# A CIN recommendation tower on one core: pair products on GpSimd, an accumulating DMA that folds eight fields, and the remainder of c out of PSUM

## The reference

```
e = jnp.stack([tbl_0[ids[:, 0]], ..., tbl_31[ids[:, 31]]], axis=1)   # 512 x 32 x 32
x0 = prev = e
for W in (filter_0, filter_1):
    z = jnp.einsum('bhd,bmd->bhmd', x0, prev).reshape(b, h * m, d)
    prev = relu(jnp.einsum('bpd,pn->bnd', z, W[0]))                  # 128 maps
    outs.append(prev)
z = jnp.sum(jnp.concatenate(outs, axis=1), axis=-1)                  # 512 x 256
h = jnp.concatenate([z, dense_ctx], axis=1)
h = jnp.maximum(h @ W_top1 + b_top1, 0.0)
h = jnp.maximum(h @ W_top2 + b_top2, 0.0)
y = h @ W_top3
```

## Time and profile before

| | |
|---|---|
| median of 3 runs | 1014.85 us (1011.53 to 1015.65) |
| the profiled execution, its own time | 1015.16 us |
| its span in the profile | 1013.4 us |
| mean granted clock of TensorE | 0.965 |
| busy: VectorE, TensorE, ScalarE, GpSimd | 962.2, 914.2, 818.3, 810.8 us |

### The profile page before, as it was taken

How to read it: one execution, slowest core, us unless ns; L and a number is a source line. 1 busy time by engine, 2 the same in 40 slices (tenths; PEclk the granted TensorE clock), 3 DMA queues, 4 the chain that set the end, 5 groups by cost and what they waited for, 6 DMA issues and landing times.

```text
span 1013.4 us, 17901 instructions
## 1 busy us (share of the span) xinstructions
PE 914.2 (90%) x3822; PEld 713.5 (70%) x3822; DVE 962.2 (95%) x1057; ACT 818.3 (81%) x2808; POOL 810.8 (80%) x452
## 2 busy tenths in 40 slices
PE   3989899898999989899999899989899988898998
PEld 2767777777778677677776777767776766677784
DVE  4899999999999999999999999999999999999993
ACT  3878888788888878788888788878888878888892
POOL 5678889788889888889888888888888788896871
PEclk9999999899999989999999899999999999999998
DMA  5412222202222202222211222211222211222000
GB/s 190 133 51 71 71 66 70 59 23 66 71 65 69 69 18 60 70 66 68 69 39 39 70 69 65 70 42 35 71 70 64 69 37 41 70 70 64 1 1 0
DMA packets 42849, 61.18 MB, mean 60 GB/s; under 512 B 6273, under 2 KB 17153, under 8 KB 42786
## 3 DMA queue, kind: packets, MB, share of 16 engines
q1 hardware_dynamic: 38690, 58.48, 18.8%
q0 software_dynamic: 4096, 2.11, 1.4%
HBM read 56.37 MB, written 4.20 MB: 60 GB/s over the span
## 4 chain that ended last, share of the span: by engine, by line
PE 61%; DVE 20%; issue 12%; ACT 3%; POOL 2%; DMA 1%; DVEq 1%; SPq 0%; ACTq 0%; POOLq 0%
PE ps_y L621 17%; PE ps_y L627 17%; PE ps_y L622 16%; DVE csum L514 6%; DVE prod L500 6%; DVE z L474 5%; PE ps_c L608 3%; PE ps_c L609 2%; PE ps_c L610 2%; ACT prod L384 2%; DVE c_lo L479 2%; PE ps_h L632 1%; POOL prod L321 1%; PE ps_c L606 1%; POOL z_lo L310 1%
## 5 line engine op out<-in xcount | busy, mean ns | idle before, releaser
L384 ACT ACTIVATE prod<-ps_y,es 128x128 f32<-128x128 f32 x2560 | 698.8, 416 | 76.2 <-PE ps_y L627 72.6
L321 POOL TENSOR_TENSOR prod<-prod 128x1536 f32<-128x1536 f32 x129 | 450.4, 3491 | 113.6 <-DVE prod L500 96.6
L627 PE MATMUL ps_y<-w_hi,c_lo 128*128 128x512 f32 x1024 | 413.4, 404 | 49.1 <-DVE c_lo L479 49.1
L621 PE MATMUL ps_y<-w_hi,c_hi 128*128 128x512 f32 x1024 | 429.2, 419 | 28.1 <-DVE prod L500 25.0
L622 PE MATMUL ps_y<-w_lo,c_hi 128*128 128x512 f32 x1024 | 411.0, 401 | 0.0
L514 DVE TENSOR_REDUCE csum<-prod 128x64 f32<-128x1280 f32 x256 | 378.2, 1478 | 10.2 <-ACT prod L384 0.6
L474 DVE TENSOR_TENSOR z<-first,second 128x512 f32<-128x512 f32 x160 | 282.1, 1764 | 7.1 <-DMA second<-et_scratch 7.1
L627 PEld LDWEIGHTS ps_y<-w_hi,c_lo 128*128 128x128 f32 x1024 | 198.7, 194 | 105.5 <-DVE c_lo L479 62.0
L500 DVE TENSOR_TENSOR prod<-ps_y,es 128x512 f32<-128x512 f32 x384 | 256.2, 677 | 10.2 <-PE ps_y L627 10.1
L621 PEld LDWEIGHTS ps_y<-w_hi,c_hi 128*128 128x128 f32 x1024 | 198.6, 194 | 94.9 <-DVE prod L500 39.1
L310 POOL TENSOR_TENSOR z_lo<-z,z_hi 128x512 fp32r<-128x512 f32 x155 | 222.3, 1452 | 6.8 <-ACT z_hi L362 6.8
(11 more groups left out here) (59 smaller groups left out, 259.0 us busy)
## 6 DMA issues: line engine op xcount, KB each, us to landing
second<-et_scratch SPq DMA_DIRECT2D x160, 256.0 KB, 4.3
first<-et_scratch SPq DMA_DIRECT2D x32, 256.0 KB, 3.3
et_scratch<-gat SPq DMA_DIRECT2D x64, 64.0 KB
prod<-w SPq DMA_DIRECT2D x4, 512.0 KB, 7.1
gat<-table,rows_now POOLq DMA_INDIRECT x128, 2.4
wt_sb<-wt SPq DMA_DIRECT2D x2, 512.0 KB, 5.5
prod<-w0a SPq DMA_DIRECT2D x1, 320.0 KB, 3.1
prod<-w0b SPq DMA_DIRECT2D x1, 320.0 KB, 3.2
```

Source lines behind the costliest of these rows:

```text
L321: nc.gpsimd.tensor_tensor(high, high, low, ALU.add).then_inc(added, 1)
L384: last = nc.scalar.activation(prod[:, buffer_of(g, u), h // 2, :, h % 2], ps_y[:, bank_of(g, u, k), j * N:(j + 1) * N], ACT.Copy, scale=es ...
L621: nc.tensor.matmul(out, hi, w_hi, start=True, stop=False)
L627: nc.tensor.matmul(out, lo, w_hi, start=False, stop=True).then_inc(y_ready, 1)
```

## The change

Four things are changed.

1. The pair products move from VectorE to GpSimd, placed by a table by tile: chunks 2 and 3 of the next group in tile 0, chunk 4 in tile 1, chunks 0 and 1 of the group after that in tile 3.
2. GpSimd's add is gone. Instead it issues one accumulating DMA a tile, `fold`, which adds fields 0 to 7 onto fields 8 to 15 within `prod`: per partition 4 KB are read and added onto 4 KB, 512 KB in all. It waits for banks 0 to 3 of the tile whose number it stands in, and signals a semaphore of its buffer.
3. The closing sum starts at field 8 and so covers 24 fields.
4. The remainder of c is computed from PSUM as max(ps_c, 0) - c_hi (`rest_c`), before `c` is written. ScalarE writes the whole `c` behind bank 6 of tile 3 (`rectify_whole`), VectorE sums it behind bank 4 of tile 0 of the next group. All of c is now in the order (u, b, d), because the matmuls of layer 1 read z's columns in that order.

```
-ADD = 12
-ADDS_LAST = ((0, 8), (8, 12))
+FOLD = F // 4
...
+        def uses_of_buffer(g, u):
+
+            return g.i * (TG * SLOTS // BUFS) + ((TG * g.r + u) // BUFS + 1)
...
-            def add(g, u, start=0, end=ADD):
...
+            def multiply(g, k):
+
+                pool.wait_ge(pairs_in[k], g.times(32, 32) if k == 0 else g.times(16, 16))
+                wait(pool, z_lo_ready, g.times(KP, k + 1 - KP))
+                nc.gpsimd.tensor_tensor(z[:, k, :], first[:, :], second[:, k, :], ALU.mult).then_inc(z_ready, 1)
+
+            def fold(g, u):
+
+                last_bank = 2 * FOLD // HB - 1
                 pool.wait_ge(act_scaled, signals(ACT_BANKS, g, u, last_bank))
                 pool.wait_ge(dve_scaled, signals(DVE_BANKS, g, u, last_bank))
+                pool.sem_inc(pool_passed, 1)
                 buf = buffer_of(g, u)
-                low, high = prod[:, buf, lows, :, :], prod[:, buf, highs, :, :]
-                nc.gpsimd.tensor_tensor(high, high, low, ALU.add).then_inc(added, 1)
+                pool.dma_start(prod[:, buf, FOLD // 2:FOLD, :, :], prod[:, buf, 0:FOLD // 2, :, :],
+                               accum_op=ALU.add).then_inc(folded[buf], 16)
...
+            Z_AT = {0: ((1, 2), (1, 3)), 1: ((1, 4),), 3: ((2, 0), (2, 1))}
+            Z_LO_AT = {0: (0, 1), 1: (2, 3), 2: (4,)}
...
                 for u in range(TG):
-                    if not (number == 0 and u == 0):
-                        add(*before(g, u))
-                    if u < 2 and (number is None or number + 1 < GROUPS):
-                        split_z(g.plus(1), 2 * u)
-                        split_z(g.plus(1), 2 * u + 1)
-                    if u == 2 and (number is None or number + 1 < GROUPS):
-                        split_z(g.plus(1), LASTK)
+                    products = (Z_AT_FIRST if number == 0 else Z_AT).get(u, ())
+                    splits = (Z_LO_AT_FIRST if number == 0 else Z_LO_AT).get(u, ()) if more else ()
+                    for n in range(max(len(products), len(splits))):
+                        if n < len(products) and (number is None or number + products[n][0] < GROUPS):
+                            multiply(g.plus(products[n][0]), products[n][1])
+                        if n < len(splits):
+                            split_z(g.plus(1), splits[n])
                     if u >= 2 and (number is None or number + SLOTS < GROUPS):
                         gather(g.plus(SLOTS), ((0, 1), (2, 3))[u - 2])
+                    fold(g, u)
...
+            def rectify_hi(g):
+
+                act.wait_ge(l0_done, g.times(1, 1))
+                nc.scalar.activation(c_hi[:, g.r, :], ps_c[:, :], ACT.Relu).then_inc(c_hi_ready, 1)
+
+            def rectify_whole(g):
+
+                act.wait_ge(c_lo_ready, g.times(1, 1))
+                act.wait_ge(h0_done, g.times(1))
+                nc.scalar.activation(c[:, :], ps_c[:, :], ACT.Relu).then_inc(c_ready, 1)
...
                         if more and (u, k) == (3, 1):
-                            rectify(g.plus(1))
+                            rectify_hi(g.plus(1))
+                        if more and (u, k) == (3, 6):
+                            rectify_whole(g.plus(1))
...
+            def rest_c(g):
+
+                dve.wait_ge(c_hi_ready, g.times(1, 1))
+                nc.vector.scalar_tensor_tensor(out=c_lo[:, g.r, :], in0=ps_c[:, :], scalar=0.0, in1=c_hi[:, g.r, :].bitcast(F32),
+                                               op0=ALU.max, op1=ALU.subtract).then_inc(c_lo_ready, 1)
...
-                    dve.wait_ge(added, g.times(TG, u + additions))
+                    dve.wait_ge(folded[buffer_of(g, u)], uses_of_buffer(g, u) * 16)
...
+                        if number != 0 and (u, k) == (0, 4):
+                            sum_h0(g)
...
                         if more and (u, k) == (3, 3):
-                            split_c(g.plus(1))
-                        if more and (u, k) == (3, 5):
-                            sum_h0(g.plus(1))
+                            rest_c(g.plus(1))
...
+                high, low = (x[:, k, :].rearrange("p (b u d) -> p u b d", u=TG, b=BT) for x in (z_hi, z_lo))
-                nc.tensor.matmul(ps_c[:, :], w0_hi[:, k, :], z_hi[:, k, :], start=(k == 0), stop=False)
-                nc.tensor.matmul(ps_c[:, :], w0_lo[:, k, :], z_hi[:, k, :], start=False, stop=False)
-                nc.tensor.matmul(ps_c[:, :], w0_hi[:, k, :], z_lo[:, k, :], start=False, stop=False)
+                nc.tensor.matmul(ps_c[:, :], w0_hi[:, k, :], high, start=(k == 0), stop=False)
+                nc.tensor.matmul(ps_c[:, :], w0_lo[:, k, :], high, start=False, stop=False)
+                nc.tensor.matmul(ps_c[:, :], w0_hi[:, k, :], low, start=False, stop=False)
```

More of the change, by code:

```diff
@@ L198, in tower @@
         dve_scaled = sem("dve_scaled")
-        added = sem("added")
+        folded = [sem(f"folded{b}") for b in range(BUFS)]
         reduced = sem("reduced")
@@ L351, in _ @@
             over_groups(pool, body)
-            add(LAST, TG - 1, *ADDS_LAST[0])
-            pool.wait_ge(added, TILES)
-            add(LAST, TG - 1, *ADDS_LAST[1])
         @block.scalar
@@ L367, in rectify @@
                 act.wait_ge(l0_done, g.times(1, 1))
-                out = ps_c[:, :].rearrange("p (b u d) -> p b u d", u=TG, b=BT)[:, :, tiles, :]
-                nc.scalar.activation(c_hi[:, g.r, :].rearrange("p (u b d) -> p b u d", u=TG, b=BT)[:, :, tiles, :],
-                                     out, ACT.Relu).then_inc(hi_ready, 1)
+                cols = slice(tiles.start * P, tiles.stop * P)
+                nc.scalar.activation(c_hi[:, g.r, cols], ps_c[:, cols], ACT.Relu).then_inc(hi_ready, 1)
                 wait(act, h0_done, g.times(1))
-                nc.scalar.activation(c[:, :].rearrange("p (b u d) -> p b u d", u=TG, b=BT)[:, :, tiles, :],
-                                     out, ACT.Relu).then_inc(ready, 1)
+                nc.scalar.activation(c[:, cols], ps_c[:, cols], ACT.Relu).then_inc(ready, 1)
+            def rectify_hi(g):
[5 more added lines that the diff above has]
+                nc.scalar.activation(c[:, :], ps_c[:, :], ACT.Relu).then_inc(c_ready, 1)
             def scale(g, u, k):
@@ L478, in split_c @@
                 dve.wait_ge(ready, g.times(1, 1))
-                nc.vector.tensor_tensor(
-                    c_lo[:, g.r, :].rearrange("p (u b d) -> p b u d", u=TG, b=BT)[:, :, tiles, :],
-                    c[:, :].rearrange("p (b u d) -> p b u d", u=TG, b=BT)[:, :, tiles, :],
-                    c_hi[:, g.r, :].bitcast(F32).rearrange("p (u b d) -> p b u d", u=TG, b=BT)[:, :, tiles, :],
-                    ALU.subtract).then_inc(lo_ready, 1)
+                cols = slice(tiles.start * P, tiles.stop * P)
+                nc.vector.tensor_tensor(c_lo[:, g.r, cols], c[:, cols], c_hi[:, g.r, cols].bitcast(F32),
+                                        ALU.subtract).then_inc(lo_ready, 1)
+            def rest_c(g):
+                dve.wait_ge(c_hi_ready, g.times(1, 1))
+                nc.vector.scalar_tensor_tensor(out=c_lo[:, g.r, :], in0=ps_c[:, :], scalar=0.0, in1=c_hi[:, g.r, :].bitcast(F32),
+                                               op0=ALU.max, op1=ALU.subtract).then_inc(c_lo_ready, 1)
             def sum_h0(g):
+                dve.wait_ge(c_ready, g.times(1, 1))
                 nc.vector.tensor_reduce(
-                    h0[:, bass.ds(g.times(TG * BT), TG * BT)].rearrange("p (u b) -> p b u", u=TG),
-                    c[:, :].rearrange("p (b u d) -> p b u d", u=TG, b=BT), AX.X, ALU.add).then_inc(h0_done, 1)
+                    h0[:, bass.ds(g.times(TG * BT), TG * BT)], c[:, :].rearrange("p (t d) -> p t d", d=D),
+                    AX.X, ALU.add).then_inc(h0_done, 1)
             def scale(g, u, k):
@@ L565, in body @@
                             reduce(*before(g, u), 0)
-                        for (n, chunk), at in (Z_AT_FIRST if number == 0 else Z_AT).items():
-                            if at == (u, k) and (number is None or number + n < GROUPS):
-                                multiply(g.plus(n), chunk)
+                        if number != 0 and (u, k) == (0, 4):
+                            sum_h0(g)
                         if number == GROUPS - 1 and (u, k) == (1, 3):
@@ L604, in layer0 @@
                     pe.wait_ge(z_lo_ready, g.times(KP, k + 1))
+                high, low = (x[:, k, :].rearrange("p (b u d) -> p u b d", u=TG, b=BT) for x in (z_hi, z_lo))
                 if k == LASTK:
[L606 removed]
+                    nc.tensor.matmul(ps_c[:, :], w0_lo[:, k, :], low, start=False, stop=True).then_inc(l0_done, 1)
                     return
[L608 to L610 removed]
+                nc.tensor.matmul(ps_c[:, :], w0_hi[:, k, :], high, start=(k == 0), stop=False)
+                nc.tensor.matmul(ps_c[:, :], w0_lo[:, k, :], high, start=False, stop=False)
+                nc.tensor.matmul(ps_c[:, :], w0_hi[:, k, :], low, start=False, stop=False)
             def layer1(g, u, k, number):
```

14 lines of the change are left out of this document (6 added, 8 removed).

## The result

| | before | changed |
|---|---|---|
| median | 1013.19 us (4 runs, 1011.14 to 1015.65) | 1092.69 us (4 runs, 1087.87 to 1098.74) |
| profiled execution / its span | 1015.16 / 1013.4 us | 1093.31 / 1091.5 us |

What follows compares the result with a forecast made beforehand. VectorE was taken as the bound, 29.2 of a 30.0 us period. Afterwards TensorE's 25.9 us a group, with head and end, gave 884.0 us; 21.7 us allowed for ScalarE's lag made 906 us, own range 886 to 928.

Steps and rivals of the forecast that it cites:

- VectorE's sum: VectorE's work a group: 29.2 us, less 8.4 for departing products, plus 2.1 for longer closing sums, giving 22.9 us.
- E: DMA engines become the bound through slow accumulation; at 7 us a fold, 34.4 us a group and 1148 us; chance 0.05.
- the 8.4 us a group: VectorE's saving from five pair products moved to GpSimd, 5 x 1.68 us.
- 1.3 was taken: Issue of the accumulating DMA on GpSimd: 1.3 us assumed, bounded above by 2.6 us.
- 5 was taken: Landing of the 512 KB fold: 5 us assumed, with ends 2.4 and 9 us.
- the cover of some 6.5 us: Between the fold's release and VectorE's closing sum, up to some 6.5 us of landing was taken as free.
- rival B: Fold lands 1 to 2 us beyond its cover, VectorE's closing sum waits; 937 to 968 us; chance 0.15.
- A: GpSimd becomes the bound if a fold's issue exceeds 1.8 us; 934 us at 2.2, 983 at 2.6; chance 0.15.
- TensorE's floor: TensorE's undisturbed matmul time: 109 long matmuls and four short pairs, 25.9 us a group.
- the 0.7: Allowance of 0.7 us a group above TensorE's 25.9 us, for ScalarE falling behind in tiles 3 and 0; 21.7 us in all.
- C: TensorE's stalls stay long enough for its clock to fall: 0.9 us more a group, 934 us; chance 0.09.
- D: Permuted columns cost layer-1 matmuls a second pass, 3.0 us a group: 999 us; chance 0.04.

Runs made afterwards that it cites:

- experiment 3: Changed kernel with the five pair products back on VectorE; fold, 24-field sum and remainder from PSUM kept: 986.41 us, 0.969 of the kernel before.
- experiment 10: Kernel before with only the remainder of c from PSUM, c's new order, permuted layer-1 columns and h0 moved: 1012.8 us, 0.9984 of the kernel before.
- experiment 4: Changed kernel with the rectification as a maximum reduction over pairs (half sum, 0), fold in place: 899.27 us, 0.8857 of the kernel before.
- experiment 2: Changed kernel without the fold's DMA, fields 0 to 7 left out of the sum, products still on GpSimd: 893.6 us, 0.8783 of the kernel before.

## Why the prediction was wrong, point by point

**The step that failed** is VectorE's sum, 29.2 - 8.4 + 2.1 = 22.9 us. It has a term for each instruction that the change touches and none for the rectification, which it doesn't touch. Measured, it grew by 7.7 us a group, so that VectorE has 30.8. With the reduction in its place VectorE was busy for 750.2 us from 30 to 878, 23.4 a group; the difference, 7.4 us, is 4 x (2.249 - 0.406). The other terms of this sum held within 0.5 us a group.

The error has two halves. I took the two-input products for the only thing on VectorE that collides with GpSimd, and said that none would be left. The section of the Trainium skill that the prediction drew on (SBUF — State Buffer, "Who interferes with whom") also names `tensor_scalar` among those that can take the shared pair; the trace agrees, and showed it beforehand: L521 spread from 201 to 724 ns with a mean of 323. Second, by the longest seen before a collision costs 0.5 us; that GpSimd's run stays closed behind a fold, for 3 to 4 us, no row of before could show, as GpSimd issued no direct transfer; so the sign of a collision could be read beforehand, its size could not. Such a wait in the place of the one removed should have been the rival on the slower side, with the point that decides it: the period passes the old 30.0 us once VectorE does, at (30.0 - 22.9)/4 = 1.8 us more on each rectification. The slower side was given to the DMA engines (E) instead, and they were idle enough.

**Part by part.** The products: moving them gives VectorE what was said, but half of the reason was misplaced. Most of what they cost above 0.68 us came from the adds of 12 fields, and with the adds gone they take 709 ns on VectorE (experiment 3), so replacing the adds alone gives 5 x (1.762 - 0.709) = 5.3 of the 8.4 us a group. Sums: 1746 ns, said 1.74 us. ScalarE's waits for z: 90.9 us, now 12.0, all of them for the first products, which VectorE still makes. Remainder of c: 681 ns, and the wait for c_lo on TensorE's weight load is down from 62.0 to 14.0 us, but only together with the rest (experiment 10). Fold: issue 0.93 us where 1.3 was taken, landing 4.5 us, and 4.9 to 5.2 in the faster kernels, where 5 was taken; VectorE waits 4.2 us in all for it, and 32.4 us in 26 waits in experiment 4. So once the rectification is short a sum does wait for the fold, about once a group, which the cover of some 6.5 us should have hidden and which was rival B's sign; it did not set the time. GpSimd: 655.8 us with long pauses, so A is off. Its two-input operations right behind a fold are some 0.35 us longer.

**The sum itself** comes out for the kernel without that wait: 25.9 + 0.7 = 26.6 us a group was forecast, and experiment 4 has (848 + 3)/32 = 26.6 and 899 us in place of 906. TensorE's floor in it is borne out. That the 0.7 fits is in part luck: it stood for ScalarE falling behind, and of its 21.7 us TensorE spends 6.3 waiting for ScalarE's scalings there, and 2.9 for VectorE's.

**The rivals.** B: the waits for the fold, 4.2 us in all, were too short to matter. C: the clock fell further than ever, 0.92 over the main part against 0.97 before, but as a consequence; in experiment 4 it is 0.99. D: refuted by experiments 2 and 10. E: the queue's share was 33.2%, and together with the loads the DMA engines were half idle.

**What the period of 32.4 us is made of:** VectorE's 30.8, and 1.6 in which it waits, mostly for TensorE (39.5 us in all on ps_y), which a rectification had stalled and whose clock then fell to the lower level.

## What to carry to other kernels

List every instruction of the engine that is to be relieved, those the change doesn't touch as well, and ask of each what GpSimd will be doing at that moment after the change; a spread in its row (201 to 724 ns) is the sign of one that collides. Where GpSimd issues a direct DMA and goes on with two-input work, a short `tensor_scalar` from SBUF on VectorE can cost the whole run; a `tensor_reduce` of twice the elements cost 0.4 us there, and a wait of GpSimd for its own operation ahead of the next opened the run. The release that starts GpSimd's run and the place of VectorE's instruction belong together: look for what stands one bank behind the release.

## What was not expected of the hardware

- **A run of GpSimd's two-input operations nearly always stays closed to VectorE's `tensor_scalar` to its end when it follows the issue of a direct DMA.** Shown: the rectification takes 2249 ns in the mean (accumulating; 80 of 81 end with the run), 1927 (plain copy; 72 of 80), 1930 (8 bytes a partition; 72 of 80), but 435 without the transfer, where it gets in between two operations. A wait between GpSimd's operations opens the run (1124 ns, none waits for two). A tiny copy behind the issue changes nothing (2336 ns); the same copy and a wait for its end bring 337 ns, mostly because the run then starts later. That the issue leaves GpSimd's parts out of step, so that there is never a moment when all are between two operations, and that a wait brings them together, is inferred; no row shows the parts, and the 8 that get in once a turn of the loop are not explained by it.
- Behind the indirect gathers no such closing was seen (27 of 27 got in behind the first operation in experiment 2).
- An accumulating DMA inside SBUF, 512 KB of fp32: issue 933 ns, landing 4.5 to 5.2 us, and 33.2% - 1.4% = 31.8% of the DMA engines' 1091.5 us for 128 of them, 2.7 us each; the plain copy 583 ns, 2.9 us, and half the engine time.
- Behind the accumulating fold GpSimd's operations last 1.6 us but start 1.25 us apart (515.47, 516.72, 517.96); behind the plain copy and the tiny one they last 1.3.
